# Mamba scan followed by neighbourhood attention: GpSimd's product with C taken over two units at a time

## The reference

```python
dt = softplus(dbl[..., :6] @ W_dt + b_dt)
Bm, Cm = dbl[..., 6:22], dbl[..., 22:38]
def step(h, inp):
    dt_t, B_t, C_t, x_t = inp
    h = exp(dt_t[:, :, None] * A) * h + (dt_t * x_t)[:, :, None] * B_t[:, None, :]
    return (h, einsum('ben,bn->be', h, C_t))
y = ys + xr * D
y = y * silu(z)
return y @ W_out
```

## Time and profile before

| | |
|---|---|
| median of 3 runs | 1130.6 us (1129.94 to 1134.67) |
| the profiled execution | 1131.42 us, its span 1129.6 us |
| PE busy | 1032.7 us (91%) |
| DVE busy | 921.2 us (82%) |
| POOL busy | 919.4 us (81%) |
| ACT busy | 566.8 us (50%) |

### The profile page before, as it was taken

The page is one execution under the profiler, slowest core; times in us unless marked ns, Lnnn a source line. Parts: engine busy times, 40 slices in busy tenths (PEclk is TensorE's granted clock), DMA queues, the critical chain, the costliest instruction groups (busy, mean ns, idle before and its releaser), DMA issues. The chain is left out here.

```text
span 1129.6 us, 9635 instructions
## 1 busy us (share of the span) xinstructions
PE 1032.7 (91%) x3278; PEld 370.6 (33%) x3278; DVE 921.2 (82%) x616; ACT 566.8 (50%) x602; POOL 919.4 (81%) x369
## 2 busy tenths in 40 slices
PE   7899998989999999999997987989999999999468
PEld 2233233333333333333332323334333333333122
DVE  1399898979999989999999899930396979989883
ACT  5766849798866666766667644320201112011212
POOL 0179999999998989999999998710298989989990
PEclk9879999999999999999999899999999999999779
DMA  3233556644556453656454756358695988946202
GB/s 89 97 135 134 201 161 172 198 160 145 192 163 182 148 174 133 178 159 221 151 191 149 186 151 213 120 120 156 128 154 95 155 150 118 168 94 98 45 1 79
DMA packets 112769, 162.78 MB, mean 144 GB/s; under 512 B 63962, under 2 KB 76992, under 8 KB 112720
## 3 DMA queue, kind: packets, MB, share of 16 engines
q1 hardware_dynamic: 109264, 155.17, 52.7%
q10 hardware_dynamic: 3456, 6.99, 2.2%
HBM read 137.43 MB, written 11.23 MB: 132 GB/s over the span
## 5 line engine op out<-in xcount | busy, mean ns | idle before, releaser
L754 POOL TENSOR_TENSOR hc<-h,c_rep 128x1024 f32<-128x1024 f32 x191 | 447.1, 2359 | 32.4 <-DVE h L807 30.0
L807 DVE TENSOR_TENSOR_SCAN h<-a,bu 128x1024 f32<-128x1024 f32 x192 | 436.6, 2283 | 24.2 <-ACT bu L635 7.2
L452 PE MATMUL y_ps<-hc,ident 128*128 128x512 f32 x768 | 374.9, 612 | 17.1 <-POOL hc L754 16.7
L625 ACT ACTIVATE a<-dt,a_neg 128x1024 f32<-128x1024 f32 x192 | 216.0, 1143 | 146.3 <-DVE h L807 116.8
L452 PEld LDWEIGHTS y_ps<-hc,ident 128*128 128x128 f32 x768 | 141.7, 192 | 218.6 <-issue 168.9
L794 DVE TENSOR_TENSOR bu<-bu,u 128x1024 f32<-128x1024 f32 x165 | 199.6, 1209 | 14.7 <-PE bu L422 12.9
L1261 POOL TENSOR_TENSOR prod_p<-vw,at 128x3584 f32<-128x3584 f32 x18 | 130.4, 7242 | 83.0 <-ACT at L1220 81.8
L1135 PE MATMUL sc_ps<-x,w_up 128*64 128x480 f32 (+3 forms) x672 | 141.1, 570 | 1.4 <-DMA x<-qk 1.4
L1135 PE MATMUL sc_ps<-x,w_low 96*64 96x480 f32 (+6 forms) x672 | 136.6, 556 | 0.0
L1208 ACT ACTIVATE sc<-sc_ps,rel 128x512 f32<-128x512 f32 x24 | 16.5, 687 | 232.8 <-PE sc_ps L1135 232.8
L422 PE MATMUL bu<-st,pick 96*128 96x512 bf16 (+1 forms) x438 | 102.7, 394 | 26.9 <-DVE h L807 23.8
(11 more groups left out here) (137 smaller groups left out, 985.1 us busy)
## 6 DMA issues: line engine op xcount, KB each, us to landing
c_rep<-bc_d SPq DMA_DIRECT2D x128, 512.0 KB, 3.8
c_rep<-bc_d SPq DMA_DIRECT2D x128, 256.0 KB, 4.0
vw<-v_d SPq DMA_DIRECT2D x24, 532.0 KB, 9.3
x<-qk SPq DMA_DIRECT2D x66, 140.0 KB, 4.5
b_rep<-bc_d SPq DMA_DIRECT2D x17, 512.0 KB, 5.0
b_rep<-bc_d SPq DMA_DIRECT2D x20, 256.0 KB, 5.1
scores_d<-sc ACTq DMA_DIRECT2D x48, 98.0 KB
at<-scores_d SPq DMA_DIRECT2D x48, 98.0 KB, 4.6
```

Of the source, the lines that this page charges most:

```text
L452: mm = pe.matmul(y_ps[:, cols(th)], ident[:, :], hc[:, k % HC_RING, cols(th)], start=(n == 0 and d == 0), stop=(n == N_ST - 1))
L625: nc.scalar.activation(a[:, k % A_RING, :], dt[:, tile % 2, :], ACT.Exp, scale=a_neg[:, kind_of(tile), n:n + 1]).then_inc(exp_done, 1)
L754: nc.gpsimd.tensor_tensor(hc[:, k % HC_RING, :], h[:, k % H_RING, :], c_rep[:, k % C_RING, :], ALU.mult).then_inc(hc_done, 1)
L807: nc.vector.tensor_tensor_scan(scan_order(h[:, k % H_RING, :], d), scan_order(a[:, k % A_RING, :], d), scan_order(bu[:, k % 2, :], d), 0.0 ...
```

## The change

`read_out` takes a first and a last unit. In the loop, an even k calls nothing, an odd k calls `read_out(k - 1, k)`: one operation on 128x2048 elements over two neighbouring slots of the three rings, which adds 2 to `hc_done` at its end. Unit 190 stays alone. That makes 95 operations of 128x2048 and one of 128x1024 out of 191 of 128x1024. The operation now waits for the later scan, for both loads of C and for PE's sum of unit `last`-4. No other line of the kernel changes.

```diff
-            def read_out(k):
-
-                pool.wait_ge(scanned, k + 1)
-                pool.wait_ge(c_in[k % C_RING], 16 * c_loads(k))
-                if k >= HC_RING:
-                    pool.wait_ge(summed, k - HC_RING + 1)
-                nc.gpsimd.tensor_tensor(hc[:, k % HC_RING, :], h[:, k % H_RING, :], c_rep[:, k % C_RING, :],
-                                        ALU.mult).then_inc(hc_done, 1)
+            def read_out(first, last):
+
+                units = range(first, last + 1)
+                pool.wait_ge(scanned, last + 1)
+                for k in units:
+                    pool.wait_ge(c_in[k % C_RING], 16 * c_loads(k))
+                if last >= HC_RING:
+                    pool.wait_ge(summed, last - HC_RING + 1)
+
+                def slots(ring, size):
+                    return ring[:, first % size:last % size + 1, :]
+
+                nc.gpsimd.tensor_tensor(slots(hc, HC_RING), slots(h, H_RING), slots(c_rep, C_RING), ALU.mult)\
+                    .then_inc(hc_done, len(units))
...
             for k in range(UNITS):
                 b_product(k + B_AHEAD)
-                if k < UNITS - 1:
-                    read_out(k)
+                if k == UNITS - 2:
+                    read_out(k, k)
+                elif k % 2 and k < UNITS - 1:
+                    read_out(k - 1, k)
                 front(k)
```

## The result

The changed kernel takes 1184.9 us (median of 4 runs, 1181.56 to 1190.48) against 1132.0 us before in the same comparison: a ratio of 1.0481, 95% interval 1.045 to 1.0512, that is 54 us slower, 51 to 58. The forecast was 1148, with a range of 1131 to 1168. The side was right, the size was not: 17 us were forecast, three times as much came, and the range was left.

A forecast was written before the change was run, and what follows sets the result against it. The prediction took DVE's scans and products with B to bound the scan stage, not POOL. 1131.4 us + 19.3 of lateness - 1.9 hidden by ACT's waits = 1148.8, put at 1148 us because the profiled execution lay above the median; range 1131 to 1168.

The forecast's parts named there:

- the ring: Ring `h`: scan of unit e+4 waits for the same pair; same lateness at another gate, so not added.
- the chain of four: POOL's chain, done 11 times: two dependent neighbours each time, about 0.05 us apiece, counted as nothing.
- the pair (12, 13): POOL's product in tile 1's preparation: forecast to end at 113.49, making DVE's product of unit 17 2.6 us late.
- tile 1: First place worked out: POOL's late pairs delay PE's sums and spreading, making DVE 3.7 us late in all.
- tile 7: Second place worked out: pair (108, 109) delays PE's sums and spreading, making DVE's product of unit 114 4.2 us late.
- the 19.3 us for the eleven preparations: Scan stage: lateness from paired products summed over the preparations of tiles 1 to 11, 19.3 us added.
- The later start: POOL's pair starts when the later scan ends; where POOL keeps up, it comes out 2.19 us later than before.
- The loads: Loads of C released together, B's behind them in SP's queue: taken as 0, bound some 4 us.
- ACT's waits: DVE's waits for ACT's copies of B, units 38 and 53: hide delays of 0.3 and 1.6 us, -1.9 us.
- The much slower one: Rival: new PE waits at seven places halve its clock, 12 us, plus 4 us of loads: 1164 us; chance 0.14.
- The two other rivals: Faster, POOL is the bound: 1118 us, chance 0.11; no difference, slack larger than counted: 1134 us, chance 0.17.

The follow-up runs named there:

- e4: Kernel before with one wait changed: PE's sum of an even unit also waits for the next unit's product; 1159.8 us, ratio 1.0245.
- e5: Kernel before with one wait changed: the scan reusing an even unit's slot of `h` also waits for the next unit's product; 1133.2 us, ratio 1.0022.
- e6: Kernel before with the three changed waits of e3, e4 and e5 together (loads, sums and ring in pairs); 1160.2 us, ratio 1.0269.
- e15: e6 plus both products of a pair made at the odd unit's place, the first also waiting for the later scan; 1190.8 us, ratio 1.0510.
- e14: Kernel before with one wait changed: POOL's product of an even unit waits for the next unit's scan; 1157.8 us, ratio 1.0233.
- e13: Changed kernel with products paired only where POOL has nothing to do between the two units (53 pairs), others alone; 1167.1 us, ratio 1.0316.
- e8: Changed kernel with loads of B issued six units ahead instead of four; 1172.5 us, ratio 1.0375.
- e9: Changed kernel with filler matmuls of zeros on PE in front of the 22 sums it waited longest for; 1180.8 us, ratio 1.0438.
- e3: Kernel before with one wait changed: SP's loads of C are released two at a time; 1138.9 us, ratio 1.0078.

## Why the prediction was wrong

**What held.** POOL wasn't the bound: with 13 us less to do it made nothing faster, as DVE's 0.5 us of waiting had said. The operation takes 4.53 us (forecast 4.54; 4.31 was the other end). The lateness travels by PE's sums: e4 alone has half of the loss, and e5 and e6 show that the ring is mostly the same lateness at another gate. (The price of 0.05 us for each dependent neighbour in the chain of four, put at nothing, is 0.11 us in the trace, a gap of 0.08 us where independent operations overlap by 0.03; with 13 of them it stays next to nothing.) Adding up POOL's work from the last idle time gave the right moment for the pair (12, 13), and at tile 1 the delay came out as 3.9 us for 3.7. That agreement is partly luck: DVE first stood at unit 15, for a sum (unit 10) that I hadn't priced, not at unit 17. At tile 7 it stood for the ring first, which I had left out of the sum as the same lateness.

**The step that failed** is the 19.3 us for the eleven preparations; the mechanism was right and the term mis-sized by about 2.5. In its place the scans lost 48 us inside the stage. The runs show three things in it.

*The later start.* I charged it as 2.19 us inside the stretches where POOL was last idle shortly before, and counted on slack to take it elsewhere. It costs 19 us on top of the rest (e15), and 26 us in e14, which also holds back the even release. e13 shows the same from the other side. The arithmetic held the scans where they were and priced a stretch as its largest lateness, with 0.3 us at tile 2 and zeros at tile 5 (PE was late by its own work), 8 (too soon for POOL to be late again) and 11. The table has 2.4, 6.4, 3.1 and 0.9 there.

*The loads, taken as 0 with 4 us as the bound.* e8 gives 12 us back. The reasoning on C was near (4.7 us of waiting); B was wrong. Its load stands behind two loads of C which are all released by one event, lands 5.6 us after its issue, and its product is due after one pair, 4.5 us. I had the three numbers, wrote them down, and took the case where POOL keeps up.

*ACT's waits, taken to hide 1.9 us.* They hid nothing: 9.1 us where they were 7.2. ACT's chain is released by scans, too, and moves with them.

**The rivals.** The much slower one came nearest in size, by the wrong mechanism. Its condition was met: the change's scan stage has 15 stretches at 0.50 with 75 us in all, against five with 24 us, and 14 of the 15 stand beside a wait of PE of over 1 us. The Trainium skill (TensorE: Matmul & The Clock Gate, Part 1) says that TensorE falls to half its clock when it has idled. The traces agree in part: of the changed kernel's 24 waits of over 1 us for a product, 11 have no such stretch beside them. But 12 us were put on it, and e9, which removed most of it, gained 4 us with overlapping intervals, net of what the fillers cost; over half of what DVE no longer waited for PE it waited for the ring instead. The two other rivals had no case.

**What stays open.** Half of e14's 23.4 us lies in one stretch, tile 7 (12.2 us), and why that one is so much dearer than the others wasn't divided further. Part of it is seen in the changed kernel, where the tile costs 11.9 us: the same pair holds DVE at the ring, PE's sum and the loads. Nor was it tried whether deeper rings would take the pairs for free, and no run separates the clock's price from that of the fillers.

## What to carry to other kernels

Fusing two small operations on an engine that isn't the bound saves little (0.14 us a pair here) and turns two releases into one late one. Before doing it, list every wait on the semaphore that it counts up, consumers and loads alike, and ask for each what was due between the two old releases; also ask what the engine was using its idle time for just ahead of its busy stretches. Where a loop of engines is coupled by short rings, a delay isn't to be priced stretch by stretch with the rest held still: one wait made later in the kernel before, a run of a single line, gives its price with everything that follows from it.

## What the hardware showed that I had not expected

Two loads of C released together land in 4.7 us by the median, where a single one took 3.8, and B's behind them in 5.6 instead of 5.0. In e3, where nothing but the loads is paired, it is 4.7 and 6.0; in e4, where they are single, 3.7 and 4.9. The granted clock does not follow a wait of PE every time: in the changed kernel's trace waits of 1.19, 1.94 and 2.57 us for a product (units 40, 76 and 26) each have a drop of 3.4 us or more beside them, and waits of 2.67 and 2.32 us (units 46 and 156) have none. And 58 us less at half clock, in e9, brought about 4 us, with overlapping intervals.
